# Turning the attention weights by DMA transposes instead of by TensorE

## The reference

```
q, k, v = split(x1 @ qkv_w + qkv_b)            # x1: [16, 128, 256], 16 heads, DH = 128
attn = einsum('bthd,bshd->bhts', q, k) * DH ** -0.5
attn = softmax(attn, axis=-1)
attn_out = einsum('bhts,bshd->bthd', attn, v)  # contracts over s
attn_out = attn_out.reshape(B, T, 2048) @ out_w + out_b
```

## Time and profile before

| | |
|---|---|
| median of 3 runs | 848.19 us (847.52 to 849.73) |
| profiled execution, own time | 849.27 us |
| its span, first to last instruction | 847.5 us |
| PE busy | 784.7 us (93%) |
| DVE busy | 581.6 us (69%) |
| ACT busy | 468.0 us (55%) |
| POOL busy | 99.9 us (12%) |

### The profile page before, as it was taken

The page is one execution under the profiler, slowest core; times in us unless marked ns, Lnnn a source line. Parts: engine busy times, 40 slices in busy tenths (PEclk is TensorE's granted clock), DMA queues, the critical chain, the costliest instruction groups (busy, mean ns, idle before and its releaser), DMA issues.

```text
span 847.5 us, 26359 instructions
## 1 busy us (share of the span) xinstructions
PE 784.7 (93%) x10276; PEld 555.8 (66%) x10276; DVE 581.6 (69%) x1547; ACT 468.0 (55%) x1556; POOL 99.9 (12%) x121
## 2 busy tenths in 40 slices
PE   6898998988988999999999998999999999888887
PEld 5676776776777666666666666666665676544433
DVE  5677777777776677777677776777767877555562
ACT  4444444444443666666666666666666667554443
POOL 1222222222221000000200002000002001011130
PEclk8878558567676999999999999999999999999999
DMA  5121211211210000000000000000000000000000
GB/s 209 41 89 42 76 40 40 78 40 41 71 35 2 2 2 0 0 0 1 0 0 0 0 0 0 0 0 0 0 0 3 2 1 2 0 1 25 25 26 25
DMA packets 6899, 19.38 MB, mean 23 GB/s; under 512 B 763, under 2 KB 3495, under 8 KB 6695
## 3 DMA queue, kind: packets, MB, share of 16 engines
q1 hardware_dynamic: 6247, 16.73, 6.1%
q10 hardware_dynamic: 576, 1.57, 0.5%
HBM read 16.20 MB, written 2.10 MB: 22 GB/s over the span
## 4 chain that ended last, share of the span: by engine, by line
PE 75%; issue 9%; DVE 7%; ACT 6%; DVEq 1%; DMA 0%; ACTq 0%; POOL 0%; SPq 0%; POOLq 0%
PE bank L352 16%; PE bank L354 16%; PE bank L353 16%; PE bank L425 11%; PE bank L372 7%; PE bank L432 5%; PE bank L575 3%; DVE h_hi L953 2%; ACT zg L720 2%; ACT nu L723 1%; DVE hid_lo L1024 1%; PE bank L359 1%; PE bank L400 1%; ACT gated L746 1%; DVE yf L1017 1%
## 5 line engine op out<-in xcount | busy, mean ns | idle before, releaser
L425 PE MATMUL bank<-h_hi,whh_hi 128*128 128x16 f16 x1536 | 112.8, 177 | 29.3 <-DVE h_hi L953 28.7
L425 PEld LDWEIGHTS bank<-h_hi,whh_hi 128*128 128x128 f16 x1536 | 92.7, 101 | 66.3 <-DVE h_hi L953 66.1
L352 PE MATMUL bank<-y_hi,w_hi 128*128 (+3 forms) x324 | 122.7, 380 | 0.0
L353 PE MATMUL bank<-y_hi,w_lo 128*128 (+3 forms) x324 | 122.6, 379 | 0.0
L354 PE MATMUL bank<-y_lo,w_hi 128*128 (+3 forms) x324 | 122.5, 379 | 0.0
L425 PE MATMUL bank<-h_hi,whh_lo 128*128 128x16 f16 x1536 | 110.6, 176 | 0.0
L718 ACT ACTIVATE zr<-bank 128x32 f32<-128x32 f32 x128 | 25.7, 201 | 130.9 <-PE bank L432 130.9
L782 ACT ACTIVATE prob<-bank,nmx 128x128 f32<-128x128 f32 x256 | 90.3, 365 | 10.8 <-DVE nmx L1034 10.8
L425 PEld LDWEIGHTS bank<-h_hi,whh_lo 128*128 128x128 f16 x1536 | 93.4, 101 | 0.3 <-issue 0.3
L1051 DVE SCALAR_TENSOR_TENSOR kT_lo<-bank,small,kT_hi 128x512 f16<-128x512 f32 x64 | 48.0, 749 | 63.5 <-ACT kT_hi L792 63.2
L354 PE MATMUL bank<-w_lo,y_hi 128*128 (+1 forms) x512 | 89.2, 219 | 0.0
(11 more groups left out here) (145 smaller groups left out, 2126.6 us busy)
## 6 DMA issues: line engine op xcount, KB each, us to landing
stage<-in_weights SPq DMA_DIRECT2D x16, 640.0 KB, 4.1
x<-in_x SPq DMA_DIRECT2D x16, 128.0 KB, 4.1
out<-yT SPq DMA_DIRECT2D x3, 512.0 KB, 2.6
adar<-in_ada_r SPq DMA_DIRECT2D x1, 1024.0 KB, 7.2
wih<-in_W_ih ACTq DMA_DIRECT2D x2, 384.0 KB, 4.2
whh<-in_W_hh ACTq DMA_DIRECT2D x2, 384.0 KB, 6.4
adaw<-in_ada_a SPq DMA_DIRECT2D x1, 512.0 KB, 8.1
out<-yT SPq DMA_DIRECT2D x4, 128.0 KB, 1.7
```

What stands on the lines that cost most here:

```text
L352: mm(ps, w[0], a[0], start=start, stop=False, skip_group_check=True)
L353: mm(ps, w[1], a[0], start=False, stop=False, skip_group_check=True)
L425: nc.tensor.matmul(out(m0 + m), half[:, k, w], h_hi[:, k * B:(k + 1) * B, 1], start=False, stop=False, skip_group_check=True)
```

## The change

PE no longer turns the weights. ACT makes the high half `p_hi` and DVE the low half `p_lo` of `pn` as it stands, in SBUF, and SP turns the eight 16-bit tiles of a step (four of each half) by eight DMA transposes into `pT_hi` and `pT_lo`. `p_T` counts 16 for each transpose, so 128 (`TURNS`) for a step. `pn`, `p_hi`, `p_lo`, `pT_hi` and `pT_lo` have one buffer each: ACT waits for the transposes of the last step before it writes `p_hi`, and SP waits for `a_mm` of the last step before it writes `pT_hi`.

```diff
+TURNS = 2 * QUAD * 16
@@ sync
+            def turn(d):
+                for part, half_ok, src, dst in ((0, p_h, p_hi, pT_hi), (1, p_l, p_lo, pT_lo)):
+                    sp.wait_ge(half_ok, d + 1)
+                    if part == 0 and d > 0:
+                        sp.wait_ge(a_mm, d)
+                    for j in range(QUAD):
+                        sp.dma_start_transpose(dst[:, j * T:(j + 1) * T], src[:, j, :]).then_inc(p_T, 16)
+
+            for d in range(NG * H):
+                turn(d)
@@ tensor, step
-                if old:
-                    pe.wait_ge(s_pn, done - 1)
-                    for j in range(QUAD):
-                        mm = nc.tensor.transpose(bank[4][:, j * T:(j + 1) * T], pn[:, u, j, :], ident[:, :])
-                    mm.then_inc(p_T, 1)
@@
                 if old:
-                    pe.wait_ge(p_l, done - 1)
+                    pe.wait_ge(p_T, (done - 1) * TURNS)
@@ scalar, step
-                if old is not None:
-                    act.wait_ge(p_T, done - 1)
-                    nc.scalar.activation(pT_hi[:, :], bank[4][:, :], copy).then_inc(p_h, 1)
@@
+                if soft:
+                    act.wait_ge(s_pn, done)
+                    if not (isinstance(done, int) and done == 1):
+                        act.wait_ge(p_T, (done - 1) * TURNS)
+                    nc.scalar.activation(p_hi[:, :, :], pn[:, :, :], copy).then_inc(p_h, 1)
@@ vector, step
-                if old is not None:
-                    dve.wait_ge(p_h, done - 1)
-                    tt(pT_lo[:, :], bank[4][:, :], pT_hi[:, :], ALU.subtract).then_inc(p_l, 1)
@@
-                    tt(pn[:, 1 - u, :, :], prob[:, :, :], rden[:, :].unsqueeze(2).broadcast_to([P, QUAD, T]),
+                    if not (isinstance(done, int) and done == 1):
+                        dve.wait_ge(p_h, done - 1)
+                    tt(pn[:, :, :], prob[:, :, :], rden[:, :].unsqueeze(2).broadcast_to([P, QUAD, T]),
                        ALU.mult).then_inc(s_pn, 1)
@@
+                if soft:
+                    dve.wait_ge(p_h, done)
+                    tt(p_lo[:, :, :], pn[:, :, :], p_hi[:, :, :], ALU.subtract).then_inc(p_l, 1)
```

More of the change, by code:

```diff
@@ L143, in build @@
         prob = sb("prob", [P, QUAD, T])
-        pn = sb("pn", [P, 2, QUAD, T])
+        pn = sb("pn", [P, QUAD, T])
+        p_hi = sb("p_hi", [P, QUAD, T], f16)
+        p_lo = sb("p_lo", [P, QUAD, T], f16)
         mx = sb("mx", [P, QUAD])
```

## The result

The changed kernel takes 1209.26 us (median of 4 runs, 1208.71 to 1210.17), the kernel before 848.35 us beside it. The ratio is 1.4253, with a 95% interval of 1.4228 to 1.4278: 361 us slower.

The account below looks back on a forecast made before the run. PE, busy 93%, was taken to bound the kernel. First weights by v at 297.6 us plus 63 loops of 11.4 gives 1015.8; with 105.6 and 1.8 around it 1123, plus 19 for the lower clock: 1142 us, range 860 to 1380.

Parts of the forecast that it names:

- What leaves PE: Four f32 transposes leave each attention step: 0.43 us, PE's own step becomes 6.57 us, 27.5 us over 64 steps.
- the room: From p_hi made on ACT to PE needing the turned weights one step later: 5.1 us.
- X: Time from when SP may issue a step's first transpose until the last of eight has landed: 10.5 us.
- the loop of X + 0.9 us: If X exceeds 5.1 us, PE waits ahead of weights by v and each step takes X plus 0.9 us.
- The work on ACT and DVE: One 128x512 operation a step leaves each engine and one equal-sized comes, taken as equal and costed at nothing.
- half of the lower clock: Weights by v at PE's lower clock adds 0.6 us a step, 38 us if always; half taken, 19 us.
- That the transposes are hidden: Rival: X within 5.1 us, one transpose each 0.49 us, PE never waits, 27.5 us gained, 822 us; chance 0.13.
- the cheaper queue: Rival: SP's transposes slower than plain DMAs but under 1.25 us each; 899 us at 0.75, 1008 at 1.0; chance 0.22.
- That they go one by one to their landing: Rival: each transpose begins only when the one before has landed, X 13.6 us, 1359 us; chance 0.20, dearer cases included.
- bound by PE at the lower clock: Rival: waits keep PE's clock low throughout, its 6.57 us step becomes 13.1 and binds, 1230 us; no separate chance.

Follow-up runs that it names:

- one instruction a half: Changed kernel with one transpose instruction turning all four tiles of a half, two issues a step instead of eight: 831.02 us, ratio 0.9796.
- one instruction a step: Changed kernel with both halves, eight tiles, in one tile and turned by one instruction after the low half is made: 830.46 us, ratio 0.9793.
- The run that fills the wait: Changed kernel with fifteen unread 512-column matmuls ahead of PE's wait for the turned weights: 1188.43 us, ratio 1.4016.
- the two-buffer kernel: Changed kernel with two buffers each for p_hi, p_lo, pT_hi and pT_lo, and a semaphore for each: 1077.13 us, ratio 1.2705.
- the last run: Kernel with one transpose instruction for each half, ACT making a group's gated output ahead of p_hi instead of behind it: 830.8 us, ratio 0.9797.

## Why the prediction was right, and where it was off

**What leaves PE, and the room.** Right. With the DMAs out of the way (one instruction a half) a step is 6.56 to 6.57 us, as the sum said. The room of 5.1 us is there too: in the step shown of that kernel SP's first issue comes as soon as `p_hi` is made, at 500.84, and PE needs the weights at 505.97, 5.13 later. With X at 3.8 us nothing waits there. With X at 6.1 to 6.2 us (four issues of transposes, or eight of copies) the steps are 7.0 to 7.2 us, which the room and the loop of X + 0.9 give alike.

**The work on ACT and DVE.** Taken as equal; `p_hi` takes 0.63 us and `p_lo` 0.69. Both stayed beside other work in the middle of a group. The sum put their new place at nothing, and there it was wrong by 1.6 us once, in the last step (below).

**X.** 10.5 us forecast, 11.2 in the median step (7 x 1.25 + 2.4), 11.3 in the mean. The spacing of 1.25 us was right as a number and wrong in its reason, which is luck. I had each transpose wait for most of the landing of the one before. In fact the issue itself holds SP's queue 1.23 us. It does so with nothing else in flight too (one instruction a step: 1.23), it stays 1.2 to 1.3 us whether an instruction carries one, two, four or eight tiles, and the DMA engines are busy for 11% only. Summed over the 16 engines, the packets took about 2.7 us for a turned tile and 2.4 for a copied one (between 350 and 650 us of the two traces). So the work in the engines, which was my reason, is not what makes a transpose dear. The landing was mis-sized, 2.4 us for 1.7.

**The loop behind X.** Forecast as "in the loop a step takes X + 0.9 us", plus 0.3 for half of the lower clock. It is 0.94 where the product meets the full clock and 1.54 where it meets the lower one, and it mostly meets the lower one. The run that fills the wait showed that this 0.6 us is the clock's. So the common step is 11.2 + 1.5 = 12.7 us against 11.4 + 0.3 forecast, and 63 x (12.75 - 11.7) = 66 us is what lies between 1142 and 1209. About 0.8 of the 1.05 us a step is X, 0.7 of it the landing, and about a quarter is the loop with its clock: I took half of the products at the lower clock, and nearly three quarters met it.

**The rivals.** That the transposes are hidden had as its condition one of them each 0.49 us; they come each 1.27, which puts out the cheaper queue (0.65 to 1.0 us each) too. It fails even for copies, at 0.64 us each. The rule of the Trainium skill that transposing DMAs are as fast as regular ones ("Advanced Engine Details and Errata", X-Bar Transpose (TRN2)) does not hold here for the time of one 32 KB tile: 2.4 us from issue to landing against 1.9, and 1.23 us of the queue against 0.60. Behind the end of the issue the two are alike, 1.2 and 1.3 us to landing; the difference is all in the issue. That they go one by one to their landing is out: in the two-buffer kernel eight took 10.17 us, where eight landings of 2.4 us would take 19. The whole program never became bound by PE at the lower clock; the mean over the attention was 0.81.

**What remains of the gain.** The forecast for hidden transposes was 822 us, the kernel with one instruction a half takes 831. The middle steps gain 0.44 us each, and the forecast had counted this gain on all 64. At the three group boundaries nothing is gained: the two steps there took 16.3 to 16.9 us together before and take 17.0. Before, on PE's timeline:

```profile
407.70 0.65 PE L575 MATMUL bank<-ident,pn 128*128 128x128 f32 x4 [1.35 <-ACT gated L746]
```

and with one instruction a half:

```profile
401.91 0.59 PE L366 MATMUL bank<-y_hi,w_hi 128*128 x1 [2.05 <-ACT gated L755]
```

PE comes sooner to its wait for the gated output, and the first products behind the longer wait run at the lower clock (0.59 us for 0.38). That `p_hi` keeps ACT 0.6 us from the gated output is part of it, but taking that away gained nothing in the end, as the last run showed. The boundaries so account for some 3.5 of the 9 us. The last group gives back the rest: its steps ahead of the last gain 2.5 us in all, about half of 0.44 each, for which no cause is shown. The last step is 9.7 us for 7.7, with a wait of PE for `aT_lo` of 4.6 us where it was 2.4. Its cause is the new place of the high half on ACT. Before, the first work of the feed-forward part followed on the last exponential, which ended at 733.81:

```profile
733.83 1.28 ACT L764 ACT_TABLE_LOAD   x1
```

With one instruction a half the last exponential ends at 713.44, ACT waits for `pn` and makes `p_hi`, and only then goes on:

```profile
714.41 0.63 ACT L804 ACTIVATE p_hi<-pn 128x512 f16<-128x512 f32 x1 [0.97 <-DVE pn L1054]
715.06 1.28 ACT L773 ACT_TABLE_LOAD   x1
...
719.14 0.39 PE L366 MATMUL bank<-aT_hi,w_hi 128*128 128x512 f16 x1 [4.56 <-DVE aT_lo L1070]
```

From this load to PE's start behind it are 4.08 us in both kernels, so the 1.6 us come through in full; the other 0.4 are what PE is earlier.

## What to carry to other kernels

Up to the eight 128x128 tiles measured here, a DMA transpose is paid by the instruction on SP's queue, not by its bytes: put all that is ready into one instruction before you judge whether it can be hidden. Compare (issues x price + landing) with the time from the moment the source is written to its use one step on; below it nothing waits, and above it every buffer without a double turns the excess into a loop with PE's product in it. With two buffers the queue was the bound, at 10.17 us for eight issues. And when an engine waits in such a loop, look at the granted clock of what it does first behind the wait.

## What the runs showed that I had not expected

- A DMA transpose from SBUF to SBUF holds SP's queue for 1.19 to 1.27 us (medians) for one, two, four and eight 128x128 tiles of 16 bits, and lands after 2.4, 2.4, 2.5 and 3.1 us. So eight tiles in one instruction cost what one costs, plus 0.7 us of landing.
- A plain copy of a 128x128 16-bit tile from SBUF to SBUF holds the queue 0.60 us; the loads of 128 KB were 0.49 apart.
- Fifteen matmuls of no use, 3.4 us a step, made the changed kernel 21 us faster.
